# One step earlier: when the query and key projections of an attention group run, beside the order of one step's small scores

## The reference, cut to what matters

```
h = layernorm(x)
q, k, v = h @ Wq, h @ Wk, h @ Wv            # 16, 4 and 4 heads
q, k = rope(q), rope(k)
scores = q @ k.T / 8, causal                # 4 query heads share a key head
a = softmax(scores) @ v @ Wo
x = x + layernorm(a)
# then: x + layernorm(a feed-forward network with 8 routed and 2 shared experts)
```

## Time and profile before

| | |
|---|---|
| median of 3 runs | 1238.08 us (1237.53 to 1239.38) |
| the profiled execution's own time | 1239.26 us |
| its span, first to last instruction | 1237.4 us |
| PE busy | 1108.4 us, 90% |
| DVE, ACT, POOL busy | 935.3, 789.5, 668.6 us |
| mean granted TensorE clock | 0.971 |

### The profile page before, as it was taken

One profiled execution on the slowest core, in us unless ns is written; L12 is line 12 of the kernel. 1 busy time (PEld: TensorE's weight loads), 2 busy tenths in 40 slices (PEclk: granted clock), 3 DMA queues, 4 the chain that ended last, 5 costly groups with the idle time before them and its releaser, 6 DMA issues.

```text
span 1237.4 us, 27070 instructions
## 1 busy us (share of the span) xinstructions
PE 1108.4 (90%) x8712; PEld 774.4 (63%) x8712; DVE 935.3 (76%) x1862; ACT 789.5 (64%) x1741; POOL 668.6 (54%) x716
## 2 busy tenths in 40 slices
PE   3799999989999997899999879999987989999996
PEld 2566666676666665766666567666664856566563
DVE  6888888847888897588888965888886466666665
ACT  3577887737787875387787655787775344444444
POOL 1375776816775774375776633776753123333332
PEclk8799999989999998999999989999998999999999
DMA  6568778754878766278788463788675111221220
GB/s 172 135 154 204 186 181 208 189 141 105 201 159 203 182 150 153 62 158 204 183 181 195 103 151 94 186 183 197 153 178 115 70 69 69 78 77 78 78 78 26
DMA packets 138813, 175.94 MB, mean 142 GB/s; under 512 B 45296, under 2 KB 133488, under 8 KB 137584
## 3 DMA queue, kind: packets, MB, share of 16 engines
q1 hardware_dynamic: 137536, 174.57, 56.8%
q10 hardware_dynamic: 1200, 0.39, 0.1%
HBM read 24.06 MB, written 2.23 MB: 21 GB/s over the span
## 4 chain that ended last, share of the span: by engine, by line
PE 53%; DVE 20%; issue 13%; ACT 11%; DMA 1%; POOL 1%; DVEq 0%; SPq 0%; ACTq 0%; POOLq 0%
PE rows L495 12%; DVE neg_max L1201 8%; PE o_out L540 6%; ACT work L784 6%; PE proj_bank L437 3%; PE small L495 3%; PE o_out L693 3%; DVE work L1224 3%; ACT probsT L793 3%; PE rows L437 2%; PE o_out L454 2%; PE rows L438 2%; PE rows L439 2%; PE proj_bank L454 2%; PE proj_bank L439 2%
## 5 line engine op out<-in xcount | busy, mean ns | idle before, releaser
L1201 DVE TENSOR_REDUCE neg_max<-rows 128x1 f32<-128x1024 f32 (+3 forms) x256 | 248.9, 1013 | 126.8 <-PE rows L498 126.1
L784 ACT ACTIVATE work<-rows,neg_max 128x1024 f32<-128x1024 f32 (+3 forms) x256 | 242.7, 952 | 140.2 <-DVE neg_max L1201 138.2
L1224 DVE STREAM_TRANSPOSE work<-work 128x896 f32<-128x896 f32 (+6 forms) x448 | 288.9, 682 | 3.0 <-ACT work L784 0.9
L540 PE MATMUL o_out<-probsT,v_g 128*64 128x128 f32 (+1 forms) x3328 | 280.2, 319 | 4.9 <-DMA probsT<-work 4.6
L540 PEld LDWEIGHTS o_out<-probsT,v_g 128*64 128x64 f32 x3328 | 203.0, 137 | 73.7 <-issue 22.3
L1044 POOL TENSOR_TENSOR attnT<-o_raw 128x256 f32 (+1 forms) x128 | 93.8, 733 | 128.2 <-ACT o_raw L800 126.8
L784 ACT ACTIVATE work<-small,neg_max 128x128 f32<-128x128 f32 (+3 forms) x256 | 133.1, 529 | 41.8 <-DVE neg_max L1209 41.7
L1012 POOL TENSOR_TENSOR turned<-turned,cf 128x512 f32<-128x512 f32 x92 | 100.6, 1093 | 77.3 <-DVE turned L1193 77.3
L1059 POOL TENSOR_TENSOR roped<-raw,cf 128x512 f32<-128x512 f32 x92 | 100.5, 1092 | 65.8 <-ACT raw L753 65.8
L495 PE MATMUL rows<-kk,qh 64*128 64x512 f32 (+2 forms) x512 | 107.7, 417 | 24.7 <-ACT probsT L793 14.0
L1068 POOL TENSOR_TENSOR roped<-roped,turned 128x512 f32<-128x512 f32 x92 | 118.9, 1292 | 13.6 <-POOL turned L1012 0.4
(11 more groups left out here) (193 smaller groups left out, 2286.2 us busy)
## 6 DMA issues: line engine op xcount, KB each, us to landing
probsT<-work SPq DMA_DIRECT2D x512, 224.0 KB, 4.1
kk<-kk SPq DMA_DIRECT2D x16, 512.0 KB, 4.6
kl<-kl SPq DMA_DIRECT2D x16, 512.0 KB, 5.6
v_g<-v_all SPq DMA_DIRECT2D x32, 256.0 KB, 3.9
probsT<-scratch SPq DMA_DIRECT2D x4, 2048.0 KB, 7.0
attnT<-scratch SPq DMA_DIRECT2D x4, 2048.0 KB, 7.0
slab_a<-w_qk SPq DMA_DIRECT2D x15, 256.0 KB, 4.1
xm<-in_x SPq DMA_DIRECT2D x4, 512.0 KB, 8.7
```

Source lines behind the costliest of these rows:

```text
L540: ins = mm(dst.rearrange("p (k c i) -> p k c i", c=QUADS, i=QUAD), v_g[p][:, t, :], x, start=t == 0, stop=t == big_w - 1)
L784: A(probs[s % 2][:, q * 128:q * 128 + width], (rows if big else turn_bank)[h][:, 0:width], ACT.Exp, bias=neg_max[:, s % 2, item:item + 1], ...
L1201: V.tensor_reduce(neg_max[:, s % 2, h:h + 1], rows[h][:, 0:big_w * 128], AX_X, ALU.max, negate=True).then_inc(max_ready, 1)
L1224: V.transpose(dst, src).then_inc(fold_done, 1)
```

## The change

`project_step` moves each projection one step ahead: k = 0 to 3 run in steps 2 to 5, k = 4 in step 7 of the group before, k = 5 in step 0. In the last group of a batch, where the next batch's tokens arrive in steps 2 and 3, k = 0 to 3 stay in steps 3 to 6, and k = 4 follows in step 7. Rotation and low part follow at lags 1 and 2 as before. Projection 4 of the very first group moves into the prologue (`project_first`, `keep_raw`). The low part of k = 3 is now made in step 7, and the small scores of step 0 stand in the order of all other steps; only in group 0 of batches 1 to 3 (`late_queries`), where k = 3 still ends in step 0, do they stay late. On SP, `load_slabs` moves to the head of step 2, ahead of `move_folds`, since `slab_a` is now read in step 2.

```diff
-def project_step(k):
-    return 3 + k if k < PROJ_A else k - PROJ_A
+def project_step(k, last):
+    return STEPS_G - 1 if k == PROJ_A else 0 if k > PROJ_A else k + (3 if last else 2)
-def projected(b, g, s):
-    return rope_index(b, g, PROJ_A + 1 + min(s, 1) if s < 3 else ROPES_G - 2 + min(s, PROJ_A + 2))
+def projected(b, g, s, last):
+    return rope_index(b, g, ROPES_G + (0 if s < 2 else min(s - (2 if last else 1), PROJ_A) + (s == STEPS_G - 1)))
-def rope_plan(b, s, lag, last):
-    out = []
-    for k in range(ROPES_G):
-        if project_step(k) + lag == s and not (last and b == B - 1 and k < PROJ_A):
-            out.append((1 if k < PROJ_A else 0, k))
+def rope_plan(b, g, s, lag, last):
+    if s < lag:
+        out = [(0, k) for k in range(PROJ_A + 1) if project_step(k, b and isinstance(g, int) and g == 0) == s - lag + STEPS_G]
+    else:
+        out = [(1 if k <= PROJ_A else 0, k) for k in range(ROPES_G) if project_step(k, last) == s - lag
+               and not (last and b == B - 1 and k <= PROJ_A)]
     return out
+def late_queries(b, g, s):
+    return b and isinstance(g, int) and g == 0 and s == 0
...
@ sync
             def load_slabs(b, g):
+                    sp.sem_inc(spacer, 1)
                     sp.wait_ge(proj_done, rope_index(b, g - 1, used))
...
             def step(b, g, s, last, depth):
+                if s == 2 and not (last and b == B - 1):
+                    load_slabs(b, g + 1)
                 if depth > 0:
                     move_folds(b, *earlier(g, s, 1))
...
-                if s == 2 and not (last and b == B - 1):
-                    load_slabs(b, g + 1)
@ tensor
-                if k == PROJ_A:
+                if k >= PROJ_A:
                     pe.wait_ge(slab_b_in, 16 * (b * HKV + g + 1))
...
-                if s:
+                if not late_queries(b, g, s):
                     score_rows(b, g, s, 0)
...
+                if depth == 0:
+                    pe.wait_ge(raw_kept, PROJ_A + 1)
...
-                if s == 0:
+                if late_queries(b, g, s):
                     score_rows(b, g, s, 0)
...
-                        pe.wait_ge(raw_kept, rope_index(b, 0, PROJ_A + 1))
+                        pe.wait_ge(raw_kept, rope_index(b, 0, ROPES_G))
...
+            project_first(PROJ_A, proj_bank[:, :])
@ scalar
+            keep_raw(0, 0, PROJ_A, proj_bank, raw[:, PROJ_A % 2, :])
@ gpsimd
-                plan = [(g + ahead, k) for ahead, k in rope_plan(b, s, 2, last)]
-                if s == 0 and not (b == 0 and isinstance(g, int) and g == 0):
-                    plan.append((g, PROJ_A - 1))
+                for ahead, k in rope_plan(b, g, s, 2, last):
+                    keep_low(b, g + ahead, k)
@ vector
-                if s:
+                if not late_queries(b, g, s):
                     small_maxima(b, g, s)
                 fold_big(b, g, s)
-                if s == 0:
+                if late_queries(b, g, s):
                     small_maxima(b, g, s)
```

More of the change, by code:

```diff
@@ L506, in turn_first @@
                 elif not at_last or b + 1 < B:
-                    pe.wait_ge(raw_kept, projected(b, g, s))
+                    pe.wait_ge(raw_kept, projected(b, g, s, at_last))
                 if not isinstance(g, int) or sigma:
@@ L571, in step @@
                     pe.wait_ge(wo_kept, 2 * b - 1)
-                if last and s == project_step(0):
+                if last and s == project_step(0, last):
                     pe.wait_ge(x_split, 2 * b + 4 if b + 1 < B else 1)
-                for ahead, k in rope_plan(b, s, 0, last):
+                for ahead, k in rope_plan(b, g, s, 0, last):
                     project(b, g + ahead, k, proj_bank)
-                if s == 0:
+                if late_queries(b, g, s):
                     score_rows(b, g, s, 0)
@@ L863, in step @@
                     keep_values(b)
-                for ahead, k in rope_plan(b, s, 1, last):
+                for ahead, k in rope_plan(b, g, s, 1, last):
                     keep_high(b, g + ahead, k)
@@ L1044, in scale_outputs @@
                 P.tensor_tensor(dst, out_t, inv_t, ALU.mult).then_inc(o_scaled, 1)
-            def low_plan(b, g, s, last):
-                plan = [(g + ahead, k) for ahead, k in rope_plan(b, s, 2, last)]
-                if s == 0 and not (b == 0 and isinstance(g, int) and g == 0):
-                    plan.append((g, PROJ_A - 1))
-                return plan
             def step(b, g, s, last, depth):
-                for ahead, k in rope_plan(b, s, 1, last):
+                for ahead, k in rope_plan(b, g, s, 1, last):
                     r, c = rope_index(b, g + ahead, k), k % 2
@@ L1060, in step @@
                                     ALU.mult).then_inc(cos_done, 1)
-                for g0, k in low_plan(b, g, s, last):
-                    keep_low(b, g0, k)
-                for ahead, k in rope_plan(b, s, 1, last):
+                for ahead, k in rope_plan(b, g, s, 2, last):
+                    keep_low(b, g + ahead, k)
+                for ahead, k in rope_plan(b, g, s, 1, last):
                     r, c = rope_index(b, g + ahead, k), k % 2
```

## The result

The changed kernel takes 1236.99 us (median of 20 runs, 1232.75 to 1240.42), the kernel before 1241.96 us on the same chip (20 runs, 1237.53 to 1245.02): a ratio of 0.9962, 95% interval 0.995 to 0.9974. It is faster, as forecast, but by 0.4% (5.0 us) instead of 0.9% (11 us). The profiled execution took 1235.35 us, 3.9 less than that of before; its span is 1233.5.

What follows compares the result with a forecast made beforehand. PE was taken as the bound. Middle groups -5.0, last groups -7.1, group 0 of batches 1 to 3 +2.0 and of batch 0 -1.5 sum to -11.6 us, giving 1227 us, range 1222.5 to 1234.5.

Steps and rivals of the forecast that it cites:

- the twin of step 4: Middle groups, step 0: with small scores in the common order PE's wait falls from 1.66 to 0.58 us, gaining 1.08.
- I cost this at nothing: Middle groups, step 1: without its projection DVE is 0.2 us behind PE, taken as free because PE has other work.
- The fold wait: Middle groups, step 3: PE waits 0 to 0.8 us, taken as 0.45, for step 1's folds, issued later behind the slabs.
- That need doesn't move: Middle groups: PE still reads step 1's last fold 13.09 us after step 1's start, having the same work before it.
- -0.9 more: Last group of each batch: projection 4 leaves its step 0, saving 0.9 us besides the 1.08 of step 0.
- I let the folds and slabs land in time: Last group of each batch: no wait on folds or slabs, as slab_a is read only in step 3.
- Nothing in batches 1 and 2: Last groups, step 7: the next batch's projection 4 costs 0.9 us in batch 0, nothing in batches 1 and 2.
- Group 0 of batch 0: First group: earlier small exponentials free the value projection's wait for `keep_raw` in step 0; -1.5 us, between -0.5 and -2.5.
- A: Rival: no new fold wait, as SP gets through sooner; middle groups gain 8.6 us, 1222.9 to 1223.5 us, chance 0.17.
- B: Rival: DMA from step 0 to step 3 is the bound, the gain returns as step 3 waits; 1232 to 1235, chance 0.18.
- C: Rival: folds land over 1.9 us later a group and the change loses; 1243 us at 2.5 us, chance 0.05.
- D: Rival: step 0's wait isn't about the small scores, so PE still waits 1.3 us there; about 1240 us, chance 0.05.

Runs made afterwards that it cites:

- small_late: The changed kernel with the small scores of step 0 late again, as in the kernel before; 1.0081 of the kernel before.
- small_only: The kernel before with only step 0's small scores and maxima in the common order (except group 0 of batches 1 to 3); 1.0065 of the kernel before.
- unroll: The changed kernel with the loop over the first three groups of a batch written out; 0.9976 of the kernel before.
- after_again: The changed kernel run and profiled once more, nothing altered; 0.9979 of the kernel before.
- v_late: The changed kernel with the second half of v_g loaded in step 3 instead of step 1; 0.993 of the kernel before, 0.9947 when repeated.
- no_slabs: The changed kernel without slab DMAs inside the steps, slabs loaded once ahead; steps 2 and 3 of a middle group together take 12.85 us.
- keys_only: The kernel before with projections 0 to 3 a step earlier and small scores in the common order, projections 4 and 5 unmoved; 0.9943 of the kernel before.
- keys_v: The kernel before with projections 0 to 3 a step earlier, small scores in common order, v_g's second half in step 3; 1224.98 us, 0.9867 of the kernel before.
- slab_bytes: The changed kernel with step 2's two slab transfers cut to 16 columns each, same issues; steps 2 and 3 of a middle group together take 13.14 us.
- v_unroll: The changed kernel with v_g's second half in step 3 and the loop over the first three groups written out; 0.9952 of the kernel before.
- before_v_loads: The kernel before with v_g's second half in step 3 and the expert weights loaded in batch 1 instead of batch 0; 1.0007 of the kernel before.

## Why the prediction was right or wrong

The direction and what makes it were right: step 0 became the twin of step 4 (wait 0.58, as forecast, where 1.66 was), PE's sum stayed, steps 6 and 7 have the forecast lengths. What failed was the sum. The middle groups gave 0.6 us of the forecast 5.0, the last groups 0.1 of the forecast 7.1, and each has three terms that stood at nothing or were sized wrong. small_late shows the order's worth by itself (0.78 a middle group at the full clock, where I had 1.08 of wait), and small_only that it hangs on the keys' move. The section on the kernel before names the reason, the low part of k = 3 made in step 0; the prediction's step 0 reads the held-back scores as an order alone and puts no condition on the gain.

*Middle groups, forecast -0.63, measured -0.08.* Three parts. The wait that step 1 was to keep, 0.23, is 0.68 in the row of 378.23; the first two parts are the 0.45 between them.

(1) "I cost this at nothing; if that cover were gone it would cost 0.2": DVE sets step 1 as soon as the projection is gone (5.49 in the last groups, 5.44 and no idle in unroll), where PE alone would need 5.29 (6.17 - 0.88). Without waits and jump the eight steps sum to 49.55, not 49.36: +0.19. "Step 2 has no wait to lengthen" was the wrong reason: a PE without waits is just the one that can't catch up.

(2) The loop's jump was not in the sum at all: +0.26 (5.75 against 5.49), and no row of mine looked at what the removed projection hid.

(3) The fold wait, 0.45 forecast: 0.53 in the profile, 0.80 in after_again: +0.08 to +0.35. The mechanism is the predicted one: v_late and no_slabs remove most of it (12.76 and 12.85 for steps 2 and 3, against 12.66 without a wait), and v_late with it a measured 0.15 to 0.5%. That its size came out near is in part luck. "That need doesn't move" was wrong: PE reads the folds 13.56 after step 1's start where nothing holds it (v_late), not 13.09, for (1) and (2) come first. And the landing is as much too late, for SP's path was mis-sized: in the fence above v_g ends at 4.32 (forecast 4.28), slab_a follows 0.72 later (0.6), slab_b 0.97 after that (0.88) and takes 0.79 (0.69), and the folds come 0.28 later (0.2): 7.08 instead of 6.65. In the mean they are issued at 7.03 and landed at 13.95, just past the late end of my 13.1 to 13.9.

*Last groups, forecast -7.1, measured -0.1.*

(1) "-0.9 more" for the departed projection counted it twice: step 0 gives 0.83 (7.55 to 6.72) and step 1 0.68 (6.17 to 5.49), 1.5 in all, for DVE sets step 1. 4 x 0.5 = 2.0.

(2) "Nothing in batches 1 and 2, where PE is busy for only 3.19 of 6.29 us" failed at both: 7.81 and 7.25 instead of 6.29, 2.5 in all. keys_only and keys_v, with projection 4 back in step 0, have 5.8 to 6.3 there. PE's idle time in that step lies ahead of its work and not beside it (timeline of PE in the changed kernel):

```profile
472.25 0.80 PE L444 MATMUL proj_bank<-xT,slab_b 128*128 128x512 f32 x1 [4.48 <-ACT probsT L803]
472.85 0.63 PE L445 MATMUL proj_bank<-xT,slab_b 128*128 128x512 f32 x1
473.27 0.63 PE L446 MATMUL proj_bank<-xT,slab_b 128*128 128x512 f32 x1
```

PE is idle until 472.25 and then has 4.71 us of work to the end, with no gap: all of the idle time is ahead of ACT's copy and none behind it. And the three matmuls of the projection, which take 0.50, 0.40 and 0.39 in a middle group, take 0.80, 0.63 and 0.63, at a granted clock of 0.56 in the step. That was to be seen in the earlier trace rows, which has a clock of 0.73. The Trainium skill says the same of the clock ("TensorE: Matmul & The Clock Gate", section "What's actually happening"): half rate is the default state and activity lifts it. The trace agrees: the first matmul after the idle time takes 0.80 us, and 0.50 at the full clock.

(3) "I let the folds and slabs land in time": in batch 0, step 4 took 9.66 instead of 6.78. PE waited 1.85 us for the folds of step 2, and the granted clock of the step was 0.82. These folds were issued behind the expert weights (SP in the changed kernel and before; then PE in the changed kernel):

```profile
205.05 1.90 SPq L390 DMA_DIRECT2D w_exp<-in_exp_w  x2
207.07 5.37 SPq L353 DMA_DIRECT2D probsT<-work  x4
```
```profile
211.21 1.33 SPq L383 DMA_DIRECT2D w_exp<-in_exp_w  x2
212.66 4.88 SPq L347 DMA_DIRECT2D probsT<-work  x4
```
```profile
217.09 3.31 PE L547 MATMUL o_out<-probsT,v_g 128*64 128x256 f32 x18 [1.85 <-DMA probsT<-work]
```

Behind the weights four fold issues take 5.37 us, and 4.88 before, where 3.49 is usual. But the order was the same before, and in unroll, slab_bytes and small_late, and none of them lost time in step 4. So the folds did not land in time here (9.75 us after step 3's start, 8.01 before), and why only in some executions stays open. The sum of the last groups: -6.0 from steps 0 and 1, +0.7 (batch 0's step 7, forecast 0.9), +2.5 and +2.9, within 0.2 of the measured -0.1.

*Group 0 of batches 1 to 3, forecast +2.0, measured +0.4.* Steps 2 to 7 do sum to 0.6 to 0.65 more each, as forecast; steps 0 and 1 swing by more than that in every kernel (step 1 took 25.1, 23.5 and 25.1 before and 23.6 three times now, and 23.5 or 25.2 in others), so no gain is to be read from them.

*Group 0 of batch 0, forecast -1.5, measured -4.5 and -2.9.* The gain of 2.9 is at the same clock in step 0, the other 1.6 is the clock's (the windows of step 0 above). Right in kind: in after_again the value projection no longer waits for `keep_raw`, and step 0 is 1.2 shorter. But step 1 is 0.8 shorter too (10.43 to 9.63), which was taken as small. small_only also has a shorter group (57.5), but at a granted clock of 1.00 in step 0, so it doesn't say how much of that is the order.

*The rivals.* A had the SP term the wrong way. B hit the number, 50.4 a group (0.9962 of 1238.08 is 1233.4, in its 1232 to 1235), but by luck and not by its reason: small_late lengthens step 0 by 0.8 and the waits stay, and slab_bytes takes bytes away and the folds land no earlier; and 0.45 of what came back is no wait in step 3 but the longer step 1 of (1) and (2). C and D didn't happen, though small_only is D in its effect: PE waits in step 0 for something else.

What stays open: keys_v still waits 0.25 us in step 2 in the mean, up to 0.9, and v_unroll 0.5; in both it is for the folds of step 0, which land late in some groups (keys_v, group 2 of batch 2):

```profile
611.31 2.18 PE L549 MATMUL o_out<-probsT,v_g 128*64 128x256 f32 x32 [0.82 <-DMA probsT<-work]
```

Why they land late in these groups and not in others, no run shows.

## What to carry to other kernels

When work is taken off an engine's path, list what it covered: another engine's step, a jump, a clock. Most of the failed terms were such covers, and each could be read in the trace before. When the order of a queue changes, count its issues and their places and not the bytes alone (here the slabs' bytes changed nothing), and move what isn't urgent (here v_g) out of the burst before putting something urgent into it. When a time that is needed and a time of landing are both forecast, check both: here both slid by about 0.4, and the wait between them looked right. And try the parts of a change singly: with v_g out of the way the keys alone were worth 1.1 to 1.3%, keys and queries together 0.5 to 0.7%.

## What the runs showed of the hardware

A slab transfer cut to 16 of its columns took about as long to issue (0.93 and 0.62 us against 0.69 and 0.79 in the rows above), and the folds behind it landed no earlier (13.91 against 13.95).

The loop's jump held TensorE's queue for 32 + 208 + 68 ns of instructions, and cost 0.26 to 0.31 us a step where no matmuls lay beside it (5.75 against 5.49 and 5.44).

After a wait PE's clock fell in some steps and not in others. The same wait of 2.05 us made one step 0 of small_only take 9.34 us, at a granted clock of 0.82 (part of it at 1.2 GHz), and another 7.94, at 1.00. A wait of 1.66 us left the clock at 1.00 in the earlier trace rows and stood in a step at 0.82 in before_v_loads. The 4.48 us of idle in step 7 above stood in a step at 0.56. So a wait can cost more than its length.
